# First experts layer: six transfers of four sorted tiles in place of one of 23

## What is computed

```python
x = x + xattn_0(layernorm(x), ctx, mask0)
x = x + experts_0(layernorm(x))        # the layer changed
x = x + xattn_1(layernorm(x), ctx, mask1)
...
def experts_0(x, Wr, br, W1, b1, W2, b2):      # E = 8 experts, H = 512, two per row
    logits = xf @ Wr + br
    topk_logits, topk_idx = jax.lax.top_k(logits, 2)
    gates = jax.nn.softmax(topk_logits, axis=1)
    dense_gates = zeros.at[arange(T)[:, None], topk_idx].set(gates)
    h = jax.nn.relu(jnp.einsum('td,edh->teh', xf, W1) + b1)
    y = jnp.einsum('teh,eho->teo', h, W2) + b2
    return jnp.einsum('te,teo->to', dense_gates, y)
```

## Time and profile before

| | |
|---|---|
| median of 3 runs | 2168.09 us (2163.49 to 2176.0) |
| span of the profiled execution, first to last instruction | 2161.6 us |
| busy share of the span | PE 86%, PEld 70%, DVE 69%, ACT 60%, POOL 29% |
| the four loads of sorted rows, issue to landing | 8.0 to 9.9 us, median 9.5 |
| idle of PE ahead of the turns, ended by these loads | 16.0 us, 4 times |

### The profile page before, as it was taken

How to read it: one execution, slowest core, us unless ns; L and a number is a source line. 1 busy time by engine, 2 the same in 40 slices (tenths; PEclk the granted TensorE clock), 3 DMA queues, 4 the chain that set the end, 5 groups by cost and what they waited for, 6 DMA issues and landing times.

```text
span 2161.6 us, 49950 instructions
## 1 busy us (share of the span) xinstructions
PE 1864.7 (86%) x17665; PEld 1517.8 (70%) x17669; DVE 1485.2 (69%) x3873; ACT 1300.1 (60%) x4466; POOL 616.4 (29%) x610
## 2 busy tenths in 40 slices
PE   3987988888889999648788989999999998898878
PEld 2776877777778777536666667777787777676765
DVE  5887776786877888566776676776767565564456
ACT  1886655565556688436677766666666654554432
POOL 0003021241312230014343434244353533333221
PEclk9998999999999999867799999999999999999999
DMA  8013334463444310210000011232222223232351
GB/s 240 17 31 102 106 114 144 130 180 96 141 128 140 102 31 7 96 64 20 24 25 2 20 39 33 83 92 66 89 62 80 82 70 105 61 96 79 99 155 51
DMA packets 119637, 178.44 MB, mean 83 GB/s; under 512 B 9824, under 2 KB 77728, under 8 KB 119136
## 3 DMA queue, kind: packets, MB, share of 16 engines
q1 hardware_dynamic: 111712, 159.51, 24.6%
q0 software_dynamic: 7680, 15.74, 2.5%
HBM read 141.26 MB, written 33.95 MB: 81 GB/s over the span
## 4 chain that ended last, share of the span: by engine, by line
PE 37%; DVE 9%; ACT 5%; issue 4%; POOL 1%; DMA 0%; DVEq 0%; ACTq 0%; SPq 0%
PE ps L1659 5%; PE ps L1944 5%; PE ps L1892 3%; PE ps L1697 3%; PE ps L1885 3%; ACT pb L2093 2%; PE ps L1681 2%; PE ps L1866 2%; PE ps L1688 2%; PE ps L1670 2%; PE ps L1707 1%; DVE nm L2472 1%; PE ps L1715 1%; PE ps L1914 1%; PE ps L1858 1%
## 5 line engine op out<-in xcount | busy, mean ns | idle before, releaser
L2093 ACT ACTIVATE pb<-ps,nm 128x128 f32<-128x128 f32 x1024 | 363.2, 377 | 194.1 <-DVE nm L2472 194.0
L2141 POOL TENSOR_TENSOR pb<-pb,rcs 128x512 f32<-128x512 f32 x256 | 267.8, 1047 | 661.6 <-DVE rcs L2480 660.8
L981 ACT ACTIVATE pb<-pb,nm 128x128 f32<-128x128 f32 x1024 | 313.0, 393 | 52.1 <-DVE nm L1206 50.6
L2497 DVE COPY pt<-ps 128x512 f32<-128x512 f32 x128 | 88.2, 689 | 198.0 <-PE ps L1944 197.9
L2093 ACT ACTIVATION_READ_ACCUMULATOR pb<-ps,nm 128x1 f32 x1024 | 221.8, 217 | 0.0
L2472 DVE TENSOR_REDUCE nm<-ps 128x8 f32<-128x1024 f32 x128 | 155.8, 1217 | 61.9 <-PE ps L1892 38.7
L1944 PE MATMUL ps<-w,pb 128*128 128x128 f32 x1024 | 168.3, 290 | 21.4 <-ACT pt L2101 10.2
L1206 DVE TENSOR_REDUCE nm<-pb 128x8 f32<-128x1024 f32 x128 | 156.1, 1220 | 4.4
L1944 PEld LDWEIGHTS ps<-w,pb 128*128 128x128 f32 x1024 | 122.2, 148 | 45.1 <-ACT pt L2101 19.3
L865 PE MATMUL ps<-w,pb 128*128 128x128 f32 x1024 | 146.0, 286 | 6.8 <-ACT pb L981 6.6
L2101 ACT ACTIVATE pt<-ps 128x512 f32<-128x512 f32 x128 | 76.9, 601 | 92.9 <-PE ps L1944 92.8
(11 more groups left out here) (379 smaller groups left out, 4415.6 us busy)
## 6 DMA issues: line engine op xcount, KB each, us to landing
big<-in_we SPq DMA_DIRECT2D x92, 514.0 KB, 3.7
big<-in_we SPq DMA_DIRECT2D x109, 384.0 KB, 3.1
sorted_out<-big SPq DMA_DIRECT2D x27, 256.0 KB
big<-sorted_in SPq DMA_DIRECT2D x7, 960.0 KB, 5.8
sorted_in<-big SPq DMA_DIRECT2D x4, 1472.0 KB, 12.2
hidden<-h_all SPq DMA_DIRECT2D x7, 512.0 KB, 3.0
h_all<-hidden SPq DMA_DIRECT2D x7, 512.0 KB, 3.8
sorted_out<-h_all SPq DMA_DIRECT2D x14, 256.0 KB
```

The source lines that it names most:

```text
L981: m = a.activation(pb[:, n % 2, k * S:(k + 1) * S], pb[:, n % 2, k * S:(k + 1) * S], ACT.Exp, bias=nm[:, n % 2, k:k + 1])
L2093: m = a.activation(pb[:, n % 2, e * S:(e + 1) * S], ps[:, score_bank(n) + half, k * S:(k + 1) * S], ACT.Exp, bias=nm[:, n % 2, e:e + 1], a ...
L2141: g_.tensor_tensor(p4, p4, r4.unsqueeze(2).to_broadcast([P, 4, S]), ALU.mult).then_inc(n2["p_normed"], 1)
L2497: v.tensor_copy(pt[:, p % 2, 4 * S:8 * S], ps[:, BANK_T, :]).then_inc(n2["p_lo"], 1)
```

## The change

`load_sorted` issues six transfers, one for each quad (five of 256 KB, one of 192 KB), in place of one. The quads take three semaphores in turn: quads 0 and 3 the first, 1 and 4 the second, 2 and 5 the third. Before it issues quad 3, 4 or 5, SP waits until quad 0, 1 or 2 of the same pair has landed. The wait that keeps the next pair from overwriting `xs0` too early is taken quad by quad. Turn q waits for its own quad. One unused semaphore is dropped.

```diff
-        group_loaded = isem("group_loaded")
+        sorted_quads = [isem(f"sorted_quad_{q}") for q in range(3)]
...
                 def load_sorted(g):
                     sp.wait_ge(moe["scattered"], 16 * 2 * PB * (g + 1))
-                    if g:
-                        sp.wait_ge(moe["xT_psum"], NQ0 * g)
-                    sp.dma_start(xs0[:, :, :], xs_d[g].rearrange("(t p) d -> p t d", p=P))\
-                        .then_inc(moe["sorted_loaded"], 16)
+                    for q in range(NQ0):
+                        first, end = quad(q, NT0)
+                        if g:
+                            sp.wait_ge(moe["xT_psum"], NQ0 * (g - 1) + q + 1)
+                        if q >= 3:
+                            sp.wait_ge(sorted_quads[q % 3], 16 * (2 * g + 1))
+                        sp.dma_start(xs0[:, first:end, :],
+                                     xs_d[g].rearrange("(t p) d -> p t d", p=P)[:, first:end, :])\
+                            .then_inc(sorted_quads[q % 3], 16)
...
-                        pe.wait_ge(moe["sorted_loaded"], 16 * (g + 1))
+                        pe.wait_ge(sorted_quads[t % 3], 16 * (2 * g + t // 3 + 1))
```

## The result

The changed kernel took 2153.99 us, the median of 11 runs (2144.0 to 2161.87), against 2168.09 for 11 runs of before (2163.49 to 2178.19). The ratio is 0.9921, with a 95% interval of 0.9900 to 0.9942: 17 us less, between 12.6 and 21.7; the two medians themselves differ by 14.1 us. A second measurement beside other runs of before gave 0.9938 (0.9914 to 0.9962), 13.4 us. The forecast was 11.8 us, ratio 0.9946.

The account below looks back on a forecast made before the run. TensorE's wait for sorted rows at turn 0 of four pairs, 16.0 us, bounds the gain; 4.2 + 3.8 + 0.2 + 3.6 = 11.8 us, so 2168.1 - 11.8 = 2156.3 us, range 2151 to 2164.

Parts of the forecast that it names:

- The landing of quad 0 at pair 0: First 256 KB at pair 0: lands 3.8 us after its issue, the median of L671's loads, ends 2.8 and 5.1.
- The clock behind turn 0 at pair 3: Turn 0 and transposes at pair 3: 1.4 us more if the clock holds; half counted, 0.7 us.
- The 3 us by which I widened the range: Whole kernel: 3 us added on each side of 2153.9 to 2160.1 for the median of a few runs.
- Pair 0, 4.2 forecast: Turn 0 of pair 0 starts at 212.9 in place of 217.08: 4.2 us gained, ends 5.2 and 2.9.
- Pair 1, 3.8 forecast: Turn 0 of pair 1: idle of 2.67 us goes, plus 1.1 us of low clock; 3.8 us, without the clock 2.7.
- Pair 2, 0.2 forecast: Turn 0 of pair 2: TensorE waits for DVE's copy instead of the load; 0.2 us gained, ends 0.9 and -0.5.
- Pair 3, 3.6 forecast: Turn 0 of pair 3: idle of 2.91 us goes, plus 0.7 us of clock; 3.6 us, ends 2.9 and 4.3.
- What is added: On SP: five more DMA issues per pair and three waits, weights of tiles 2 and 3 issued later; costs nothing.
- the 8.3 at which it was to cost: SP's hold per pair, 6.1 us expected; from 8.3 us each microsecond costs one. Slower rival, chance 0.04.
- The 2 us to spare: Pair 1: weights there at 351.7 with the longest landing, wanted by TensorE at 353.9, so in time by 2 us.

Follow-up runs that it names:

- the later runs: Both kernels measured again, unedited: the kernel before at 2166.39 us (ratio 0.999) and 2177.55 us, the changed kernel at 2153.86 us (0.9938) and 2161.93 us.
- The early copy: Against the changed kernel, DVE copies the turned gates ahead of the mask and the maximum at pair 2's turn 0; 2153.57 us, ratio 0.9935.
- two transfers: Against the changed kernel, quad 0 and then the other 19 tiles in place of six transfers, SP waiting for no landing; 2156.22 us, ratio 0.9921.
- the run of pairs 1 to 3 alone: Against the changed kernel, pair 0 loads its rows in one transfer and only pairs 1 to 3 in six; 2161.86 us, ratio 0.9958.

## Why the prediction fell short

**What failed.** The mechanism held; two terms of the sum were too small. The landing of quad 0 at pair 0 stood at 3.8 us and took 2.9, so 5.3 us were gained there in place of 4.2. The clock behind turn 0 at pair 3 stood at 0.7 us and gave about 2.2, so 5.1 us were gained in place of 3.6. With them, and less of pair 1 kept, the four places gave 12.8 us in place of 11.8, and the whole stage 14.2 in that profile. The 3 us by which I widened the range did not cover what the ratio shows beyond that; the cause of that rest stays open.

**Where the time goes.** Right: the gain is made at the four turns, and the wait for a sixth of the rows in place of all is what gains (six transfers waited for as a whole: 0.999, 0.9959 to 1.0021).

**Pair 0, 4.2 forecast, 5.3 measured (4.7 to 5.1 in the later runs).** The term was mis-sized by the landing of quad 0: I took L671's median of 3.8 us, and it took 2.9 (207.96 to 210.88). The lower end of the rows, 2.8, was the right one: SP had issued nothing for 11 us before. At pairs 1 to 3, right behind a weight load, quad 0 took 3.9 to 4.4 us in the three profiles of the change. By the fit of the Trainium skill, page "DMA: Bandwidth & Descriptors", section "Anatomy of one DMA", the estimate was 2.6 us; at 256 KB and pair 0 the trace agrees within 0.3 us. The section gives that fit for transfers issued from GpSimd, and SP issues these. At 1472 KB it gives 5.5, where the loads of the three profiles of before took 7.7 to 12.3 us, so it does not hold for these loads at that size.

**Pair 1, 3.8 forecast, 4.4 measured, 2.6 kept.** The idle went and the clock stayed high over turn 0. What I had not counted is hidden 0, 1.13 us in place of 1.73, and that the clock fell 7 us later and took 1.8 us back.

**Pair 2, 0.2 forecast, -0.2 measured.** Right in the mechanism, as named: DVE's copy became the wait, 3.80 us of idle in place of 3.26. The early copy, which gains there, shows that it was the copy.

**Pair 3, 3.6 forecast, 5.1 measured.** The clock was the term: I counted half of it, it did not fall, and hidden 0 behind the transposes, which I had left out of that sum, ran at full clock too, 1.13 us in place of 1.91. The idle of 2.91 us itself was right. That the clock may fall there was right: in two other profiles with pair 3 split it did, and the place gave 3.6 us (two transfers) and 3.7 (the early copy), where with a high clock it gave 5.1. Turn 0 and what follows it there, two transfers:

```profile
609.25 0.60 PE L743 MATMUL ps<-w,big 128*128 128x128 f32 x4
609.69 1.85 PE L867 MATMUL ps<-w,pb 128*128 128x128 f32 x8
```

So the whole price of the clock was too small as well: 1.4 us left hidden 0 out.

**What is added, nothing.** Right in the three profiles of the change: SP was held 7.1 us at pair 1 in the first, and none of the hidden products 0 to 3 behind the turns of pairs 1 to 3 waited for weights. The margin is thin: in the run of pairs 1 to 3 alone, at a hold of 7.8 us, below the 8.3 at which it was to cost, hidden 2 of pair 1 did wait for its weights. The 2 us to spare had been reckoned with TensorE 7.4 us behind the issue, and there it came after 4.9.

**The base and the range.** The sum was made against one profile, in which TensorE waited 8.8 us for the loads of pairs 1 to 3; in the third profile it was 12.5. A wait that depends on a transfer in a shared queue should have had a range of its own. And 3 us for the spread of medians was too little where single runs spread over 27 us with the granted clock. Together the stage gained 14.4 us on average over three profiles each, which lies in the intervals of both measurements (12.6 to 21.7, and 8.2 to 18.6 us).

What stays open: why the load of pair 2 takes 8.5 us in one execution and 12.3 in another, since the trace doesn't tell the DMA engines apart (it is not the chip: on each of the two chips of the later runs it took 8.5 or 8.6 us once and 12.3 once); and whether the rest up to the 17 us of the first measurement is more than its uncertainty.

## What to carry to other kernels

Where a consumer starts with the first part of a large load and is late for it, give that first part a transfer and a semaphore of its own, ahead of the rest; here two transfers did as well as six. Price it as the idle that goes, then look at each place for who is next in line, and count the clock behind an idle as part of its price. Take the length of a wait from more than one execution.

## What the runs showed of the hardware

One load of 1472 KB on SP's queue took 7.7 to 8.0 us with the queue to itself, in all three profiles of before, and 8.5 to 12.3 us between weight loads. A first transfer of 256 KB landed after 2.7 to 2.9 us at pair 0, with 1216 KB right behind it as with two more of 256 KB; one of 768 KB landed after 4.95 us. Right behind a weight load of 514 KB, at pairs 1 to 3, the 256 KB took 3.8 to 4.4 us. The time of one and the same kernel follows the mean granted clock of TensorE: 27 us of 2170 between 0.958 and 0.945.
